# A new time table that puts the local and the global sums of a windowed-attention kernel side by side

## The reference

```python
x = x + layernorm(attention(layernorm(x)))       # 2 x 8192 tokens, 512 features, 16 heads of 32
x = x + layernorm(fourier_ffn(layernorm(x)))     # real(ifft(fft(x) @ w)) + bias, a 512x512 product

# attention, for each head
logits = einsum(q, k of three neighbouring blocks of 64) * scale      # masked to 64 keys around the query
out_local = softmax(logits) @ v
lg = einsum(q, k[:, ::64]) * scale                                    # 128 global keys
out_global = softmax(lg) @ v[:, ::64]
out = (out_local + out_global) @ w_out + b_out
```

## Time and profile before

| | |
|---|---|
| time, median of 3 runs | 3414.16 us (3412.81 to 3414.69) |
| the profiled execution's own time | 3419.38 us |
| its span, first to last instruction | 3417.6 us |
| granted TensorE clock, mean | 0.987 of full speed |
| busy over the span | PE 98%, PEld 73%, DVE 73%, ACT 58%, POOL 56% |

### The profile page before, as it was taken

How to read it: one execution, slowest core, us unless ns; L and a number is a source line. 1 busy time by engine, 2 the same in 40 slices (tenths; PEclk the granted TensorE clock), 3 DMA queues, 4 the chain that set the end, 5 groups by cost and what they waited for, 6 DMA issues and landing times.

```text
span 3417.6 us, 72834 instructions
## 1 busy us (share of the span) xinstructions
PE 3338.3 (98%) x24916; PEld 2508.1 (73%) x24916; DVE 2491.0 (73%) x4425; ACT 1993.9 (58%) x3876; POOL 1915.6 (56%) x2961
## 2 busy tenths in 40 slices
PE   8999999999999699999999999999999999999997
PEld 6888888888888467777777777777777777777775
DVE  4444544445444578988898888988898889888986
ACT  2222322222222567777777777777777777777772
POOL 0000000000000378888788878888888878887885
PEclk9999999999999689999999999999999999999999
DMA  7778778787788656766667666776676666766651
GB/s 186 234 207 242 220 215 239 209 239 223 207 240 239 140 107 142 161 148 142 142 146 160 138 138 144 165 159 139 142 161 148 142 142 149 159 140 137 144 133 38
DMA packets 538325, 572.77 MB, mean 168 GB/s; under 512 B 55752, under 2 KB 354344, under 8 KB 538024
## 3 DMA queue, kind: packets, MB, share of 16 engines
q1 hardware_dynamic: 457992, 533.97, 62.6%
q10 hardware_dynamic: 79744, 34.70, 5.7%
q0 software_dynamic: 288, 0.20, 0.1%
HBM read 330.98 MB, written 203.23 MB: 156 GB/s over the span
## 4 chain that ended last, share of the span: by engine, by line
PE 58%; DVE 5%; POOL 2%; issue 1%; ACT 1%; ACTq 0%; POOLq 0%; DVEq 0%
PE ps_misc L1215 18%; PE ps_mx L1111 9%; PE ps_sc L1133 7%; PE ps_os L1167 5%; PE ps_os L1186 5%; PE ps_os L1192 4%; PE ps_sc L1152 3%; PE ps_os L1199 3%; PE ps_sc L1224 2%; DVE qk L1007 1%; PE ps_os L1170 1%; DVE bnb L989 1%; DVE r_loc L1033 1%; PE ps_sc L1121 1%; DVE r_glob L1033 1%
## 5 line engine op out<-in xcount | busy, mean ns | idle before, releaser
L1007 DVE TENSOR_REDUCE qk<-ps_mx 128x10 f32<-128x640 f32 x1024 | 809.4, 805 | 130.3 <-PE ps_mx L1111 119.1
L962 ACT ACTIVATE ps_mx<-mask 128x640 f32<-128x640 bf16 x1022 | 715.1, 706 | 124.3 <-DVE qk L1007 113.1
L520 PE MATMUL po<-ht_hi,w_both 128*128 128x512 f32 x2048 | 639.0, 391 | 1.5 <-ACT ht_hi L302 1.5
L933 ACT ACTIVATE qk<-ps_sc 128x384 f32<-128x384 f32 (+1 forms) x1024 | 443.4, 459 | 298.0 <-PE ps_sc L1133 242.6
L520 PEld LDWEIGHTS po<-ht_hi,w_both 128*128 128x128 f32 x2048 | 385.3, 188 | 86.3 <-issue 4.1
L883 POOL TENSOR_SCALAR_AFFINE_SELECT qk<-qk 128x512 f32<-128x512 f32 (+1 forms) x512 | 317.6, 620 | 233.1 <-ACT qk L933 228.0
L520 PE MATMUL po<-ht_lo,w_both 128*128 128x512 f32 x1024 | 399.2, 390 | 0.0
L886 POOL TENSOR_SCALAR_AFFINE_SELECT qk<-qk 128x512 f32<-128x512 f32 x512 | 335.3, 655 | 35.0
L524 PE MATMUL po<-w_both,ht_hi 128*128 128x512 f32 x1024 | 320.6, 389 | 1.3 <-DVE w_both L371 1.3
L946 ACT ACTIVATE v<-ps_sc 128x512 f32<-128x512 f32 x512 | 297.0, 593 | 33.3 <-PE ps_sc L1152 33.3
L893 POOL TENSOR_TENSOR qk<-qk 128x256 f32<-128x256 f32 x384 | 290.8, 767 | 10.7
(11 more groups left out here) (159 smaller groups left out, 7843.0 us busy)
## 6 DMA issues: line engine op xcount, KB each, us to landing
xb<-in_L_attn_x SPq DMA_DIRECT2D x256, 256.0 KB, 6.3
w_both<-q_hi_d SPq DMA_DIRECT2D x256, 256.0 KB
q_lo_d<-o_lo SPq DMA_DIRECT2D x32, 1024.0 KB, 8.6
k_lo_d<-o_lo SPq DMA_DIRECT2D x32, 1024.0 KB, 10.1
w_both<-q_lo_d SPq DMA_DIRECT2D x128, 256.0 KB
vw<-v_d SPq DMA_DIRECT2D x128, 256.0 KB, 5.0
out<-xb SPq DMA_DIRECT2D x128, 256.0 KB, 3.2
bt<-at ACTq DMA_DIRECT2D x496, 64.0 KB, 6.0
```

The source lines that it names most:

```text
L520: last = nc.tensor.matmul(po[bank(o, u)][:], wa[:, k, o * P:(o + 1) * P], ha[u][:, k, :], start=start, stop=stop)
L933: nc.scalar.activation(p_loc[:, tile, 2 * hp:2 * hp + 2, lo:MW], ps_sc[n % 2][:, 0:2 * MW].rearrange("p (h n) -> p h n", h=2)[:, :, lo:MW] ...
L962: nc.scalar.activation(ps_mx[u % 2][:, :, 0:MWG], mask[:, turn:turn + 1, :].to_broadcast([P, 2, MWG]), ACT.Copy).then_inc(seeded, 1)
L1007: nc.vector.tensor_reduce(mb[s % 2][:, heads, tile, :], ps_mx[u % 2][:, :, 0:MWG].rearrange("p h (b n) -> p h b n", n=WIN), axis=AX.X, op= ...
```

## The change

Only the numbers of the table change, with one effect on the kind of neighbours: `sg` gets a time 0.001 after `sl`, so that they always follow each other. All items, their shapes and their waits are what they were.

```diff
-        PERIOD = 16.5
+        PERIOD = 16.2
         STEP = {
...
-            "sl": (17.694,),
-            "sg": (17.911,),
...
+            "sl": (15.231,),
...
+            "sg": (15.232,),
         }
...
```

More of the change, by code:

```diff
@@ new lines, in attention_phase @@
+            "max": (-29.977, -23.829, -17.833, -16.48, -16.792, -19.668, -17.41, -8.925),
+            "maxr": (-23.789, -19.101, -15.469, -15.272, -23.078, -12.076, -12.97, -11.58),
+            "seed": (-26.795, -18.453, -15.132, -18.293, -16.413, -10.747, -9.5, -4.24),
+            "maxc": (-10.809,),
+            "mt": (-7.996,),
+            "x_mt": (-10.557,),
+            "loc": (0.56, 2.011, -0.863, 3.018, -1.206, 0.454, 10.805, 10.737),
+            "x_loc": (9.319, 5.546, 2.312, 4.301, 1.247, 13.389, 5.485, 8.635),
@@ new lines, in attention_phase @@
+            "locm": (-1.243, -0.837, 4.214, 10.337),
+            "sadd": (0.63, 12.029, 11.494),
+            "last": (2.193,),
+            "x_last": (9.327,),
+            "lastm": (3.168,),
+            "glob": (5.072, 12.275, 3.019, 12.494),
+            "x_glob": (15.855, 9.375, 4.396, 6.165),
+            "ol": (13.885, 13.033, 13.768),
+            "oc": (15.129,),
+            "sl": (15.231,),
+            "sums": (19.074,),
+            "pvgo": (18.465,),
+            "rglob": (21.071,),
@@ L759, in attention_phase @@
+            "ogm": (23.678,),
+            "rloc": (20.64,),
+            "olm": (20.138,),
+            "osum": (22.952,),
+            "sg": (15.232,),
         }
         BY_GROUP = {
-            "ot": (50.7, 28.42, 45.746, 14.118),
-            "otl": (53.185, 27.844, 37.238, 32.356),
+            "ot": (45.549, 37.16, 46.408, 16.214),
+            "otl": (61.264, 26.817, 26.828, 28.796),
         }
         TILE = {
-            "out": (23.041, 21.305, 24.153, 22.556, 32.588, 28.022, 27.217, 27.949, 40.453, 39.05, 41.896, 35.968, 42.451, 45.411, 40.17, 44.177),
@@ L766, in attention_phase @@
[L766 to L780, removed]
+            "out": (17.059, 19.443, 16.969, 21.235, 30.644, 25.459, 27.41, 27.858, 33.372, 37.642, 43.238, 33.094, 42.983, 40.994, 35.822, 43.455),
@@ new lines, in attention_phase @@
+            "outa": (22.337, 32.926, 37.832, 44.526),
+            "outs": (24.667, 34.199, 40.867, 46.787),
+            "rs0": (28.909, 25.179, 45.443, 42.376),
+            "x1": (29.76, 35.606, 42.069, 50.445),
+            "x1s": (30.104, 36.079, 46.884, 51.937),
+            "rs1": (33.506, 28.863, 45.578, 51.191),
+            "x1n": (35.611, 44.648, 49.673, 61.115),
+            "tr": (40.084, 46.587, 56.549, 63.308),
+            "x_tr": (39.422, 47.303, 60.327, 63.313),
+            "trl": (40.27, 49.712, 56.166, 66.397),
@@ L781, in attention_phase @@
+            "ffn": (55.664, 53.548, 50.551, 47.026, 59.773, 60.192, 57.52, 59.092, 66.429, 65.834, 68.83, 71.982, 76.896, 76.125, 79.419, 76.975),
+            "ffna": (55.414, 64.587, 70.91, 82.662),
+            "ffns": (78.525, 58.061, 83.239, 67.415),
+            "rs2": (64.226, 82.006, 77.458, 70.039),
+            "za": (80.008, 84.904, 92.189, 75.859),
         }
```

## The result

The changed kernel takes **3492.7 us** (3489.9 to 3495.55) where the kernel before, on the same chip, takes 3414.43. The ratio is 1.0225, with a 95% interval of 1.0213 to 1.0237: 2.25% slower, where 1.4% faster was forecast.

What follows compares the result with a forecast made beforehand. The prediction took PE's own sequence and its few waits to bound the kernel. Its terms, -27 - 14 - 21 + 3 + 0 + 8 = -51 us, took 3414.2 to 3363, shaded by 3 to 3366 us; range 3347 to 3398.

Steps and rivals of the forecast that it cites:

- The wait of `mt`: PE's waits at `mt` for DVE's join, 0.75 a chunk, vanish behind `max` 0 and a `tr`: -21 us (-5 to -23).
- The merge: On PE, `sg` directly behind `sl` saves a change between matmul kinds, 0.21 a step: -27 us (-14 to -43).
- `ol`, -14: At PE's `ol`, the mask from POOL is ready 0.63 earlier, so a wait of 0.15 goes: -14 us (0 to -20).
- Added: Costs on PE: +3 for lone `tr`, 0 for `mt` and `tr` following a shorter matmul, +8 for new small waits.
- `tr` and the entries: On PE, lone `tr` pay another way out, +3 us; `mt` and `tr` following a 320-column matmul, 0, at most +13.
- Rival C: At PE's `max` 2, `seed` 0 from ACT is late: 3416 us, or 3441; chance 0.08 slower, 0.04 about the same.
- Rival B: Only the sums' gain on PE; waits of `ol` and `mt` return elsewhere: 3390 us (3384 to 3406), chance 0.20.

Runs made afterwards that it cites:

- a_rglob: The changed kernel with only `rglob` moved behind the join on DVE, two-input join kept: 3499.63 us, ratio 1.0242 to the kernel before.
- aj_rglob: The changed kernel with the one-input join and also `rglob` moved behind the join on DVE: 3391.95 us, ratio 0.9926 to the kernel before.
- a_join1: The changed kernel with the join's last step (L1020) as a reduction of one input instead of two: 3385.87 us, ratio 0.9911 to the kernel before.
- a_olm64: The changed kernel with POOL's `olm` on only 64 of 512 columns, the other products left out: 3379.6 us, ratio 0.989 to the kernel before.
- a_olm: The changed kernel with only `olm` moved ahead of `lastm` on POOL, two-input join kept: 3409.33 us, ratio 0.9983 to the kernel before.
- a_olmlate: The changed kernel with `olm` moved behind the third `locm` on POOL, two-input join kept: 3402.27 us, ratio 0.9958 to the kernel before.
- aj_unmerged: The changed kernel with the one-input join and `sg` back behind `loc` 1, undoing the merge: 3404.83 us, ratio 0.9958 to the kernel before.
- a_unmerged: The changed kernel with `sg` back behind `loc` 1, undoing the merge, two-input join kept: 3514.04 us, ratio 1.0284 to the kernel before.

## Why the prediction was wrong

The step that failed is "The wait of `mt`". It says that 0.68 of PE's work now lies in front of a wait of 0.50, "Both should vanish", and takes -21 with bounds of -5 and -23. Measured: PE idle for 0.76 at each `mt`, +97 us, and 0.93 (3.71 a chunk, 118 us) from start to start against the kernel in which the join is on time. The step moved PE's side and kept DVE's: it assumed that the join comes no later than before. Its own caution, the `rglob` ahead of the join, is about DVE's queue, and the runs on it (a_rglob, aj_rglob) showed that this is not the reason. The reason lies in neither queue: L1020 and POOL's `olm` and mask don't run side by side, and the new table puts the three together in each step. Taking DVE's second input away or shortening POOL's `olm` frees the time (a_join1: 107 us; a_olm64: 113, with some POOL work left out), and changing their order on POOL frees most of it (a_olm: 83, a_olmlate: 90). In the trace of before there was a hint: the row at `mt` named L1020, whose durations spread from 184 to 404 ns for a fixed shape, the long ones beside a mask of POOL's; POOL's order around it was not looked up, as `mt` was read as a matter of PE and DVE alone.

The other terms are best judged in a_join1, where this wait is gone.

- **The merge, -27 (-14 to -43).** Right in each distance of the timeline, and as a whole 19 us by the medians of aj_unmerged and a_join1 (16 by their ratios), 25 by the length of their chunks (69.01 and 68.23), 21 by a_unmerged against the changed kernel.
- **`mt`, -21.** With the one-input join all waits of `mt` are gone: 0.70 a chunk before (read start to start as the next point's, 0.50 and 0.20), 22 us. The size was right for the kernel in which the join is on time.
- **`ol`, -14.** In the changed kernel it happened (5.9 us left of 32.9), but only as PE was late anyway. With `mt` in time it came back: 23.3 us, in 50 steps of 106 instead of nearly all. Half the steps take 1.40 and half 1.70 to 1.72, 0.6 a chunk too much, no less than before. `x_loc` 7 does end earlier as forecast; POOL's own queue, on the critical chain now with 16%, makes the mask late: in a_olm64, where POOL has less to do and PE isn't held up at `mt`, this wait is 5.3 us. The passage "the mask can be ready 0.63 earlier" looked at ACT alone. So 0 instead of -14.
- **Added.** `tr` and the entries can't be told apart from the rest. New small waits stand at `loc`: start to start, against the shortest distance between matmuls of the same kinds, 0.25 a chunk between `loc` and `loc` and 0.17 between `max` and `loc`, together 13 us, for +8.
- **The sum** with these: -25 - 22 - 0 + 3 + 13 = -31. The profiled executions differ by 34 (spans of 3417.6 and 3383.4), the medians by 29.
- **Rival C** (seed 0 late for `max` 2) did not come: in the changed kernel and in a_join1 no row of PE itself waits for L962 (its weight loads do, for 46.4 and 53.2 us, less than the 94.4 before). Rival B was the nearest to a_join1, with other parts: there the wait of `mt` went and that of `ol` stayed. None of the rivals looked for an instruction that takes longer for the same work.

**What stays open.** The merge in the old table: that its loss comes from the `loc` wait (67 us by one timeline, two thirds of the 100 to account for) is read from rows and not shown by a run, as the two runs that moved this wait only turned it into others. Why a_olmlate, in which no row has `mt` waiting for L1020, is still 16 us above a_join1: 0.3 of its 0.5 a chunk stands in front of `mt`, the rest in front of `out`, `ffn` and `loc`. And why one POOL instruction lets the waiting DVE instruction in and another doesn't, below.

## What to carry to other kernels

When a table or a scheduler moves work, read the durations on the other engines too, not only their order: an instruction of a few elements that sits between two engines may have a fixed shape and no fixed time. Before you move a DVE instruction with two SBUF inputs on which the bound engine waits, list what POOL does in its neighbourhood; if it's back-to-back elementwise work, either give it one input (here 107 us, at no cost in the kernel before) or change POOL's order. And a merge on PE is worth what its rows say (about 20 us) only with something between the `loc` that follow it.

## What the hardware showed that was not expected

A DVE instruction held by POOL's is not always served next. In the step from 1563.22 of the changed kernel, on DVE and on POOL:

```profile
1563.22 2.13 DVE L1020 TENSOR_TENSOR qk<-qk 128x16 f32<-128x16 f32 x1
```

```profile
1563.06 0.42 POOL L889 TENSOR_SCALAR_AFFINE_SELECT p_last<-p_last 64x256 f32<-64x256 f32 x1
1563.45 1.26 POOL L897 TENSOR_TENSOR o_loc<-o_loc,r_loc 128x512 f32<-128x512 f32 x1
1564.68 0.62 POOL L883 TENSOR_SCALAR_AFFINE_SELECT qk<-qk 128x512 f32<-128x512 f32 x1
1565.37 0.64 POOL L886 TENSOR_SCALAR_AFFINE_SELECT qk<-qk 128x512 f32<-128x512 f32 x1
```

L1020 began during L889 and had to stand through L897 and L883, both of which began after it; it ended at 1565.35, before L886, which waits for a semaphore of L883's and leaves a gap. In eleven of the kernels here (1500 to 3290) I counted the cases in which L1020 is held while one POOL instruction ends and the next has begun. From L897 to the mask L883 it was passed over in 298 of 298, from L889 to L883 in 75 of 75, from L889 to the full L897 in 75 of 75. But it got in, some 40 ns after the end of the one, in all 202 cases from L897 to L889 in which it had asked more than 0.1 us before (in 48 more it asked within the last 40 ns, with L889 begun, and stood through L883 too), in 40 of 40 from L886 to L897, in 26 of 26 from L889 to the L897 of 64 columns, and in 75 of 75 from L886 to the 128x1 instruction L875. The next instruction starts 22 to 62 ns before the end of the one before in all of these, with held and admitted cases at 23 and at 47 alike, so that the overlap doesn't tell them apart, and no run here does. What such a hold costs is clear, though: one or two further POOL instructions, 0.6 to 1.9 us, for a DVE instruction of 0.19.
